# Seven quads of routed rows turned by loads from SBUF to SBUF, and expert outputs written to two PSUM banks in turn

## The chip, the core and the metric

The kernel is one program on 1 core of a Trainium2 chip. The metric is device time in microseconds (us), from one launch to its end. Each kernel is run several times, and the median counts.

The engines are TensorE (PE; PEld is its weight loads), VectorE (DVE), ScalarE (ACT), GpSimd (POOL) and SyncE (SP), which here only issues DMAs. Each engine takes its own instructions in order and waits on semaphores. A name with a q behind it (SPq) is that engine's queue of instructions that start DMAs or set registers.

## What is computed

The input x is 32 sequences of 125 tokens of 192 numbers. The reference does three things in a row:

- It scores each token (a product with `tok_w`) and keeps the best 88 of 125 in each sequence, in order of score: 32 x 88 = 2816 rows.
- It adds quantized attention of the layer-normed rows: q, k and v from one matrix, 12 heads of 16, scores quantized to steps, a softmax that gives powers of two, a projection, all of it rounded to steps.
- It adds a mixture of experts of the layer-normed rows: they are normed once more and scaled, a gate picks 4 of 16 experts for each row with softmax weights, each expert is 192 -> 384 -> gated unit -> 192, and the four outputs are summed with their weights.

Float products are made from fp16 pairs, a high part and the rest (low part), so one product takes several matmuls.

## The kernel before, in words

**Front part** (about 0 to 130 us). x is loaded, scored, ranked, and gathered into `xsel` (24 tiles of 128 rows, `NT` = 24; three tiles are a *quad* of four sequences, `NQ` = 8). Meanwhile SP fills `region` in DRAM with empty rows (`fill_rows`, L480 to L484: 45 stores of 800 KB) and loads the weights of experts two by two (`load_pair`, L464 to L478). SP's order is written out at L493 to L499: for m from 2 to 8 it issues some fills, waits on `stage_low` and loads pair m. The last 11 fills belong to m = 4.

**Attention part** (to about 445 us). It is a pipeline of slots, one per tile (`tile_slots`, `slot(st, n, q)` in each engine's program). In a slot, DVE runs the softmax of one tile (L1381 to L1466), ACT its half of it (L961, L988, L1009, L1015), PE the scores of the next tile and the output of the one before. Work for whole quads hangs in certain slots: q, k and v of the next quad, and behind it the routing of the quad that is through attention. For quad q the routing steps sit in slots 3q+5 (`COEFFS`) to 3q+9 (`SEND`):

- `NORM`, slot 3q+6: ACT writes the normed rows as fp16 high parts into `rows[q % 3]` (L894, L899).
- `TURN`, slot 3q+7: POOL adds the low parts (`low_rows`, L335 and L336, semaphore `low2`). PE then turns the rows by nine transposes of 128x128 into PSUM, in two lots (`turn_rows`, L1715 to L1724: two tiles, then one). DVE copies each lot to `xTr` in SBUF (`evac_rT`, L1294 to L1303). ACT copies 64 of its partitions to `tEr` (`last_rows`, L901 to L906).
- `GATE`, the same slot, at its end: PE makes the gate's logits from `xTr` and `tEr` with 15 matmuls (`gate_rows`, L1726 to L1738). DVE picks the four experts (`top_experts`, L1305 on, its first instruction is L1309).
- `RANK` and `SEND`: the place of each row in its expert's list, and 12 indirect stores per quad from POOL, each of which writes the rows of one tile and one choice to `region`.

PE's matmuls for q, k, v, turning and gate all use PSUM bank `pX` one after another. The order is made by `fill_order` (L345 on): fill n may start when drain n-1 is through (`xr_filled`, `xr_drained`). In a `TURN` slot the order is: turn lot 0, turn lot 1, `("qk", 4)`, gate, `("qk", 5)`. ACT drains a `qk` fill with L878, and in its program the drain of `("qk", 4)` stands behind `last_rows`. It has L1009, the softmax step that DVE's next slot needs, right behind that. Quad 7 (`LASTQ`) is turned inside the expert part, through bank `pO`.

**Expert part** (to about 726 us). Rows of `region` are taken in 59 steps (`NS`) of 256 rows of one expert, again as a pipeline of slots (`step_slots`). In slot st:

- SP loads step st: a transposing load of 256 x 384 numbers of 2 bytes from DRAM (L527) and a small load (L529), up to 8 steps ahead.
- PE makes the hidden values of step st-2 in three groups of five matmuls (L1904: hidG, hidC, hidL), then the output of step st-5 in ten (L1920) into `y_ps`, one half of bank `pX`.
- ACT starts with moving the output of step st-6 out of `y_ps` (L1044, semaphore `y_out`), then applies the gating function (L1049, L1052), then makes fp16 parts (L1059, L1061) and copies `tEb` (L1067) for later steps.
- DVE clips and multiplies (L1593, L1600), makes low parts (L1577, L1578), and computes where rows go. POOL scatters the output rows to `expert_rows` by two indirect stores per step (L782).

PE waits before L1920 until the output before has left the bank (L1915: `y_out` >= p - 5), and before the first L1904 of a step for `te_copied`, `l_done` (DVE's L1593) and `gs_ready` of two steps earlier (L1896 to L1898).

**Last part.** `expert_rows` is loaded back, weighted, summed and stored.

Of the kernel before, what the change touches and what calls it, by code (L numbers as in the profile page):

```python
# [64 lines left out]
def audio_tower(nc, x, tok_w, tok_b, w_qkv, b_qkv, w_proj, b_proj, sw_qkv, sw_proj, s_a1, s_attn,  # L65
                s_a2, s_a3, ffn_scale, gate_w, gate_b, w1, b1, w2, b2, out):
    ctx = ExitStack()
    with ctx:
# [19 lines left out]
        def carve(shape, dt, size):  # L88
# [212 lines left out]
        y_ps = pX[:, 0:2 * C].rearrange("p (j c) -> p j c", j=2)  # L301
# [9 lines left out]
            dve_chain root2 var2 ssq2 base_ready shift2 norm2 high2 low2 tT_drained ter_copied coeffs  # L311
# [36 lines left out]
        def fill_order():  # L348

            order = []  # L350
            for st in range(LAST):
                i, nxt = st % 3, st // 3 + 1 < NQ
                if nxt:
                    order += [(st, "qk", 1)] if i == 1 else [(st, "v", 0)] if i == 2 else [(st, "x", 0), (st, "x", 1)]
                    order += [(st, "qk", 2), (st, "qk", 3)] if i == 1 else []
                if nxt and i != 1:
                    order += [(st, "x", 2)] if i == 0 else [(st, "v", 1)]
                if quad_at(st, RANK) is not None:
                    order += [("rank", quad_at(st, RANK))]
                if quad_at(st, TURN) is not None:  # L360
                    order += [("rows", quad_at(st, TURN), m) for m in range(2)]
                if nxt and i == 1:
                    order += [(st, "qk", 4)]
                if quad_at(st, GATE) is not None:
                    order += [("gate", quad_at(st, GATE))]
                if nxt and i < 2:
                    order += [(st, "qk", 5 * i)]
            return {name: 11 + n for n, name in enumerate(order)}
# [26 lines left out]
        def turned(q):  # L395

            return rT_ps if q < NQ - 1 else rT_last

# [16 lines left out]
        ROUTE_CONSTS = 38  # L415
        WIDEN_AT = 2
# [13 lines left out]
        def _(sp):  # L430
# [62 lines left out]
            sp.wait_ge(s["route_consts"], ROUTE_CONSTS)  # L493
            for m in range(2, E // 2 + 1):
                for f in range(*((0, 24) if m == 2 else (24, 34) if m == 3 else (34, NFILL) if m == 4 else (0, 0))):
                    fill_rows(f)
                if m < E // 2:
                    sp.wait_ge(s["stage_low"], 12 * (m - 1))
                    load_pair(m % 2, 2 * m)  # L499

# [294 lines left out]
        def _(act):  # L795
# [105 lines left out]
            def last_rows(q):  # L901

                act.wait_ge(s["tT_drained"], 2 * q + 2)
                if q >= 1:
                    act.wait_ge(s["xr_filled"], fill("gate", q - 1) + 1)
                act.activation(tEr[0:CB, :], xTr[0:CB, 2, :], ACT.Copy).then_inc(s["ter_copied"], 1)  # L906
# [130 lines left out]
            def gate_values(st, p, it):  # L1037
                r, u = st % 2, st % UNROLL
                b = (st - 6) % 4
                if active(st, 6):  # L1040
                    act.wait_ge(s["mm2_done"], p - 5)
                    if st >= 10:
                        act.wait_ge(y_sent[b], it * 64 + 32 * ((u - 6) // 4))
                    act.activation(ysb[b], y_ps, ACT.Copy, scale=1.0 / (XS * WS * WS)).then_inc(s["y_out"], 1)  # L1044
# [50 lines left out]
        def _(dve):  # L1095
# [198 lines left out]
            def evac_rT(q, m):  # L1294

                dve.wait_ge(s["xr_filled"], fill("rows", q, m) + 1)
                if q >= 1:
                    dve.wait_ge(s["ter_copied"], q)
                dst = xTr[:, :, 0:256] if m == 0 else xTr[:, :, 256:384]
                dve.tensor_copy(dst, turned(q)[m]).then_inc(s["xr_drained"], 1)  # L1300
                if m == 1:
                    dve.wait_ge(s["xr_drained"], fill("rows", q, m) + 1)
                    dve.sem_inc(s["tT_drained"], 2)  # L1303
# [71 lines left out]
            def slot(st, n, q):  # L1375
# [60 lines left out]
                if quad_at(st, TURN) is not None:  # L1436
                    evac_rT(quad_at(st, TURN), 0)
# [5 lines left out]
                if quad_at(st, TURN) is not None:  # L1443
                    evac_rT(quad_at(st, TURN), 1)
# [177 lines left out]
        def _(pe):  # L1622
# [92 lines left out]
            def turn_rows(q, m):  # L1715
# [3 lines left out]
                for i in ((0, 1), (2,))[m]:  # L1719
                    src, cols = rows[q % 3][:, i, :], slice(128 * (i % 2), 128 * (i % 2) + 128)  # L1720
                    for kind, lo in enumerate((0, 2 * CA, CA)):
                        ins = pe.transpose(turned(q)[m][:, kind, cols], src[:, lo:lo + 128], idh[:, :])
                ins.then_inc(s["xr_filled"], 1)

            def gate_rows(q):

                pe.wait_ge(s["ter_copied"], q + 1)
                pe.wait_ge(s["tT_drained"], 2 * q + 2)
# [4 lines left out]
                for i in range(3):  # L1733
                    cols = slice(128 * i, 128 * i + 128)
                    for n, (lhs, kind) in enumerate(((xTr[:, 0, cols], 0), (xTr[:, 0, cols], 1), (xTr[:, 1, cols], 0),
                                                     (xTr[:, 2, cols], 2), (tEr[:, cols], 3))):
# [38 lines left out]
            def slot(st, n, q):  # L1775
# [34 lines left out]
                if quad_at(st, TURN) is not None:  # L1810
                    for m in range(2):
                        turn_rows(quad_at(st, TURN), m)
# [77 lines left out]
            def products(st, p, it):  # L1890
# [16 lines left out]
                if active(st, 5):  # L1907
# [5 lines left out]
                    pe.wait_ge(s["ave_ready"], p - 4)  # L1913
                    if st >= 6:
                        pe.wait_ge(s["y_out"], p - 5)  # L1915
                    for j in range(2):
                        tok = slice(128 * j, 128 * j + 128)
                        for n, (lhs, kind) in enumerate(((av[g][:, 0, tok], 0), (av[g][:, 0, tok], 1), (av[g][:, 1, tok], 0),
                                                         (av[g][:, 2, tok], 2), (avE[g][:, tok], 3))):
                            ins = pe.matmul(y_ps[:, j, :], lhs, w2s[:, kind, bass.ds(k_, 1), :].rearrange("p o f -> p (o f)"),  # L1920
# [45 lines left out]
```

## Time and profile before

| | |
|---|---|
| runs | 757.69, 760.58, 761.43 us; median 760.58 |
| the profiled execution: its own time | 765.98 us |
| its span (first to last instruction) | 764.2 us |
| mean granted TensorE clock | 0.685 |
| busy, share of the span | DVE 73%, ACT 64%, POOL 59%, PE 58% |
| chain that ended last, by engine | PE 22%, ACT 18%, SPq 17%, DVE 17%, issue 12%, another core or an unknown queue 6%, POOL 4% |
| DMA queues | SP's 139266 packets, 75.04 MB; POOL's 10272 packets, 17.70 MB |

Busy is the time in which an engine had an instruction under way. "Idle before" an instruction is put down to whatever released it ("<-"); "issue" means that the profile shows no wait. The granted clock is 1.00 at full speed and 0.50 at half. The sum of the prediction is made against the profiled execution, and its difference is applied to the median.

### The profile page before, as it was taken

What the parts mean: (1) busy time and instruction counts of PE and PEld (TensorE: products, weight loads), DVE (VectorE), ACT (ScalarE), POOL (GpSimd) and SP (SyncE); (2) the same over time, 40 slices, a digit from 0 to 9 for tenths busy, and PEclk for the clock granted to TensorE, in tenths of its full rate; (3) what the DMA queues carried; (4) which work ended last, traced back from release to release, by engine and by line L of the source; (5) the groups of instructions that cost most, each with busy time, mean ns of one, the idle gap of its engine ahead of it and who ended that gap; (6) DMA issues with size and microseconds to landing.
All of it is one profiled execution on the core that took longest, in us unless ns stands there. A gap on an engine that the chain in (4) does not pass through costs nothing.

```text
span 764.2 us, 14352 instructions
## 1 busy us (share of the span) xinstructions
PE 441.1 (58%) x3943; PEld 294.3 (39%) x3943; DVE 560.7 (73%) x1426; ACT 490.9 (64%) x874; POOL 447.3 (59%) x554
## 2 busy tenths in 40 slices
PE   0695353746456463745633335567687787788454
PEld 0242132333334242433422224345465565466343
DVE  3686897899999999898998645545676665666746
ACT  0055876798897969788774535255666655666664
POOL 9781725247587987979777653555455444445500
PEclk9997555555555555555555567679999988979669
DMA  9469999999011030210101164425444344431078
GB/s 186 55 145 293 318 318 294 321 293 285 13 55 53 22 93 30 79 40 6 51 11 40 52 102 86 101 72 126 97 92 93 83 95 86 91 81 34 1 291 317
DMA packets 149613, 93.65 MB, mean 123 GB/s; under 512 B 77122, under 2 KB 143643, under 8 KB 149538
## 3 DMA queue, kind: packets, MB, share of 16 engines
q1 hardware_dynamic: 139266, 75.04, 38.7%
q0 software_dynamic: 10272, 17.70, 7.3%
q8 instruction: 36, 0.59, 0.3%
q14 instruction: 39, 0.32, 0.2%
HBM read 23.61 MB, written 61.24 MB: 111 GB/s over the span
## 4 chain that ended last, share of the span: by engine, by line
PE 22%; ACT 18%; SPq 17%; DVE 17%; issue 12%; another core or an unknown queue 6%; POOL 4%; DMA 2%; DVEq 0%; ACTq 0%; POOLq 0%
SPq L483 7%; PE pX L1920 6%; PE pS L1904 6%; PE pP L1904 4%; SPq L475 3%; POOL w1s L597 2%; DVE S_e L1462 2%; ACT stage L1059 2%; DVE negmx L1381 2%; SPq L537 2%; DMA w2s<-expert_rows 2%; SPq L432 2%; PE pP L1796 1%; ACT stage L1044 1%
## 5 line engine op out<-in xcount | busy, mean ns | idle before, releaser
L782 POOL DMA_INDIRECT expert_rows<-stage,dest x118 | 118.6, 1005 | 130.3 <-ACT stage L1044 74.4
L1593 DVE TENSOR_SCALAR arena<-pS 128x512 f32<-128x512 f32 x59 | 40.6, 689 | 80.7 <-remote 59.9
L1920 PE MATMUL pX<-w2s,stage 128*128 x472 | 65.1, 270 | 39.8 <-ACT stage L1044 32.1
L706 POOL DMA_INDIRECT region<-rows,slots x60 | 68.0, 1134 | 16.5 <-issue 15.9
L597 POOL TENSOR_TENSOR w1s<-stage,w1s 128x384 f16<-128x384 f32 (+8 forms) x72 | 67.3, 935 | 11.4 <-ACT w1s L866 6.4
L1920 PEld LDWEIGHTS pX<-w2s,stage 128*128 128x128 f16 x472 | 43.6, 106 | 57.3 <-issue 53.6
L1052 ACT ACTIVATE arena<-pS 64x256 f32<-64x256 f32 x59 | 22.1, 375 | 59.5 <-PE pP L1904 30.1
L1796 PE MATMUL pP<-idb,S_p 128*88 128x128 bf16 x192 | 25.8, 316 | 46.3 <-DVE S_p L1414 46.3
L1674 PE MATMUL pX<-arena,WA 128*128 128x384 f16 x86 | 34.4, 501 | 30.5 <-ACT arena L878 21.2
L1823 PE MATMUL pP<-WpT,oq 128*128 128x192 bf16 x72 | 15.4, 349 | 60.7 <-ACT pTs L996 57.7
L706 POOL DMA_INDIRECT region<-arena,slots x36 | 41.0, 1138 | 15.6 <-issue 8.5
L961 ACT ACTIVATE S_g<-S_w,kf 128x1056 int16<-128x1056 uint16 x24 | 30.3, 1264 | 23.5 <-DVE S_w L1386 23.5
L752 POOL CAST oq<-o 128x384 bf16<-128x384 int8 x24 | 20.8, 865 | 41.3 <-ACT o L971 41.3
L1904 PE MATMUL pS<-arena,w1s 128*128 128x256 f16 x224 | 38.2, 293 | 8.3 <-issue 8.2
L878 ACT ACTIVATE arena<-pX,qkB,qkA 128x384 int8<-128x384 f32 x43 | 28.6, 665 | 22.1 <-PE pX L1674 16.3
L1044 ACT ACTIVATE stage<-pX 128x384 f32<-128x384 f32 x59 | 27.9, 473 | 22.6 <-remote 16.3
L1462 DVE SCALAR_TENSOR_TENSOR S_e<-S_sq,kf,S_pow 128x1056 f32<-128x1056 f32 x24 | 33.6, 1398 | 11.9 <-ACT S_sq L988 9.8
L1796 PEld LDWEIGHTS pP<-idb,S_p 128*88 128x88 bf16 x192 | 21.9, 191 | 51.6 <-DVE S_p L1414 49.5
L1049 ACT ACTIVATE arena<-pP 128x256 f32<-128x256 f32 x59 | 21.9, 371 | 26.9 <-remote 19.3
L1697 PE MATMUL pS<-arena 32*96 32x88 bf16 (+1 forms) x576 | 33.3, 276 | 7.6 <-ACT S_u L886 4.0
L1904 PE MATMUL pS<-tEb,w1s 128*128 128x256 f16 x118 | 35.4, 300 | 3.8 <-issue 3.8
L1422 DVE SCALAR_TENSOR_TENSOR S_rho<-S_g,kf,S_w 128x1056 int16<-128x1056 int16 x24 | 35.7, 1486 | 1.1 <-ACT S_g L961 1.1
(442 smaller groups left out, 1620.7 us busy)
## 6 DMA issues: line engine op xcount, KB each, us to landing
region<-zrow SPq DMA_DIRECT2D x45, 800.0 KB
w1s<-expert_rows SPq DMA_DIRECT2D x16, 384.0 KB, 7.7
stage<-in_L_ffn_w_dram SPq DMA_DIRECT2D x24, 192.0 KB
stage<-in_L_ffn_w_dram SPq DMA_DIRECT2D x8, 384.0 KB
w2s<-expert_rows SPq DMA_DIRECT2D x8, 384.0 KB, 11.8
arena<-in_x_dram SPq DMA_DIRECT2D x4, 672.0 KB
expert_rows<-stage,dest POOLq DMA_INDIRECT x118
out_dram<-xsel SPq DMA_DIRECT2D x8, 198.0 KB
```

Of the source, the lines that this page charges most:

```text
L483: sp.dma_start(region_rows[FILL * f:FILL * f + FILL].rearrange("(p j) c -> p j c", p=128), zrow[:, 0:ROW].unsqueeze(1).broadcast_to([128, ...
L597: pool.tensor_tensor(ws[rows, min(kind + 1, 3), two, to:to + width], st[rows, :, at:at + width], ws[rows, kind, two, to:to + width], ALU.s ...
L706: pool.indirect_dma_start(region_rows, bass.IndirectOffsetOnAxis(ap=slots[q % 3][:, i, m:m + 1], axis=0), rows[q % 3][:, i, :].bitcast(I16 ...
L782: pool.indirect_dma_start(y_dram, bass.IndirectOffsetOnAxis(ap=dest[(st - 7) % 8][:, j:j + 1], axis=0), ysb[b][:, j, :], None, bounds_chec ...
L1044: act.activation(ysb[b], y_ps, ACT.Copy, scale=1.0 / (XS * WS * WS)).then_inc(s["y_out"], 1)
L1422: dve.scalar_tensor_tensor(S_rho[:, :, :], S_g[:, :, :], k(K_X), S_w[:, :, :], ALU.mult, ALU.subtract).then_inc(s["rho_ready"], 1)
L1462: dve.scalar_tensor_tensor(S_e[:, :, :], S_sq[:, :, :], k(K_KK), S_pow[:, :, :].bitcast(BF16), ALU.add, ALU.mult).then_inc(s["e_ready"], 1)
L1593: dve.tensor_scalar(lin[r], hidLC[r], -6.0 * XS * WS, 8.0 * XS * WS, ALU.max, ALU.min).then_inc(s["l_done"], 1)
L1674: ins = pe.matmul(bank[:, 0:384], W[:, 128 * c:128 * c + 128], xT[:, kind, :], start=kind == 0, stop=kind == 2)
L1796: ins = pe.transpose(pP[0:KEEP, 0, 128 * h:128 * h + 128], S_p[:, h, :].bitcast(BF16), idb[:, :])
L1904: ins = pe.matmul(dst, w1s[:, kind, bass.ds(k_, 1), 128 * window:128 * window + 128].rearrange("p o f -> p (o f)"), rhs, start=n == 0, sto ...
L1920: ins = pe.matmul(y_ps[:, j, :], lhs, w2s[:, kind, bass.ds(k_, 1), :].rearrange("p o f -> p (o f)"), start=n == 0, stop=n == 4)
```

## The change

1. **Turning.** For quads 0 to 6 PE's nine transposes and DVE's two copies are dropped. In their place SP issues three transposing loads from `rows[q % 3]` in SBUF to `xTr` in SBUF, one per tile of 128 rows and 384 columns (`turn_by_load`). SP waits for `low2` first. In SP's program the call for quad m-4 stands ahead of the load of expert pair m (for m from 4 to 8), and the last two stand behind that loop. ACT's `last_rows` and PE's `gate_rows` wait on the new semaphore `turned` in place of `tT_drained`. The fills of `pX` for turning drop out of the order. Quad 7 stays as it was.
2. **Layout.** The loads write the columns in their order, so the second and third plane of `xTr` change places everywhere.
3. **Two banks.** The expert output of step n goes to bank `pO` for odd n from 7 on, and to `pX` otherwise. From step 8 on PE waits for `y_out` of the output before the last (p - 6), not of the last. Step 7 also waits until quad 7 is through with `pO` (`own_ready` >= 2).

```diff
+        y_banks = [bank[:, 0:2 * C].rearrange("p (j c) -> p j c", j=2) for bank in (pX, pO)]
+        def y_ps(n):
+            return y_banks[n % 2 if n >= Y_APART else 0]
...
-                if quad_at(st, TURN) is not None:
+                if quad_at(st, TURN) is not None and quad_at(st, TURN) == NQ - 1:
                     order += [("rows", quad_at(st, TURN), m) for m in range(2)]
...
+        Y_APART = SPREAD_AT
...
+            def turn_by_load(q):
+                sp.wait_ge(s["low2"], 2 * q + 2)
+                if q >= 1:
+                    sp.wait_ge(s["xr_filled"], fill("gate", q - 1) + 1)
+                    sp.wait_ge(s["ter_copied"], q)
+                for i in range(3):
+                    sp.dma_start(xTr[:, :, 128 * i:128 * i + 128], rows[q % 3][:, i, 0:2 * C],
+                                 transpose=True).then_inc(s["turned"], 16)
             for m in range(2, E // 2 + 1):
                 for f in range(*((0, 24) if m == 2 else (24, 34) if m == 3 else (34, NFILL) if m == 4 else (0, 0))):
                     fill_rows(f)
+                if m >= 4:
+                    turn_by_load(m - 4)
                 if m < E // 2:
                     sp.wait_ge(s["stage_low"], 12 * (m - 1))
                     load_pair(m % 2, 2 * m)
+            for q in range(E // 2 - 3, LASTQ):
+                turn_by_load(q)
...
             def last_rows(q):
-                act.wait_ge(s["tT_drained"], 2 * q + 2)
+                if q < LASTQ:
+                    act.wait_ge(s["turned"], 48 * q + 48)
+                else:
+                    act.wait_ge(s["tT_drained"], 2)
                 if q >= 1:
                     act.wait_ge(s["xr_filled"], fill("gate", q - 1) + 1)
-                act.activation(tEr[0:CB, :], xTr[0:CB, 2, :], ACT.Copy).then_inc(s["ter_copied"], 1)
+                act.activation(tEr[0:CB, :], xTr[0:CB, 1, :], ACT.Copy).then_inc(s["ter_copied"], 1)
...
-                    act.activation(ysb[b], y_ps, ACT.Copy, scale=1.0 / (XS * WS * WS)).then_inc(s["y_out"], 1)
+                    act.activation(ysb[b], y_ps(st - 6), ACT.Copy, scale=1.0 / (XS * WS * WS)).then_inc(s["y_out"], 1)
...
-                if quad_at(st, TURN) is not None:
-                    evac_rT(quad_at(st, TURN), 0)
...
-                if quad_at(st, TURN) is not None:
-                    evac_rT(quad_at(st, TURN), 1)
...
             def gate_rows(q):
                 pe.wait_ge(s["ter_copied"], q + 1)
-                pe.wait_ge(s["tT_drained"], 2 * q + 2)
+                if q < LASTQ:
+                    pe.wait_ge(s["turned"], 48 * q + 48)
+                else:
+                    pe.wait_ge(s["tT_drained"], 2)
...
-                if quad_at(st, TURN) is not None:
-                    for m in range(2):
-                        turn_rows(quad_at(st, TURN), m)
...
+                    if st - 5 == Y_APART:
+                        pe.wait_ge(s["own_ready"], 2)
                     if st >= 6:
-                        pe.wait_ge(s["y_out"], p - 5)
+                        pe.wait_ge(s["y_out"], p - 5 if st - 5 <= Y_APART else p - 6)
...
-                            ins = pe.matmul(y_ps[:, j, :], lhs, w2s[:, kind, bass.ds(k_, 1), :].rearrange("p o f -> p (o f)"),
+                            ins = pe.matmul(y_ps(st - 5)[:, j, :], lhs, w2s[:, kind, bass.ds(k_, 1), :].rearrange("p o f -> p (o f)"),
```

## Rows read from the trace of the kernel before

**Rows 1.** Table of stretches: us; busy us of each engine (instructions); PEclk, DMA, GB/s

```profile
190.00:445.00 255.00, 128.21 (x1508) 84.09 (x1508) 226.56 (x463) 193.74 (x271) 195.92 (x213) 0.50 0.14 42
517.00:712.00 195.00, 150.79 (x1195) 109.82 (x1193) 119.52 (x320) 122.57 (x286) 97.03 (x97) 0.91 0.40 86
```

**Rows 2.** Timeline in the TURN slot of quad 2: start us, us, engine, line, idle before

```profile
270.39 1.10 POOL L336 TENSOR_TENSOR rows<-tn,rows 128x384 f16<-128x384 f32 x1
...
271.54 0.82 PE L1722 MATMUL pX<-idh,rows 128*128 128x128 f16 x6
...
272.40 0.56 DVE L1300 COPY early<-pX 128x768 f16<-128x768 f16 x1 [0.70 <-PE pX L1722]
...
273.62 0.36 DVE L1300 COPY early<-pX 128x384 f16<-128x384 f16 x1 [0.40 <-PE pX L1722]
...
274.07 0.52 ACT L906 ACTIVATE tEr<-early 64x384 f16<-64x384 f16 x1 [0.67 <-issue]
...
274.29 1.50 DVE L1462 SCALAR_TENSOR_TENSOR S_e<-S_sq,kf,S_pow 128x1056 f32<-128x1056 f32 x1 [0.31 <-DVE early L1300]
...
275.21 0.67 ACT L878 ACTIVATE arena<-pX,qkB,qkA 128x384 int8<-128x384 f32 x1 [0.62 <-PE pX L1674]
...
276.20 0.27 PE L1737 MATMUL pX<-gws,early 128*128 128x16 f16 x4
...
276.60 0.17 PE L1737 MATMUL pX<-gws,tEr 128*128 128x16 f16 x1
...
277.00 0.20 DVE L1309 COPY arena<-pX 128x48 f32<-128x48 f32 x1
```

**Rows 3.** Timeline of SP's first loads of steps and of ACT's use of them

```profile
444.61 1.36 SPq L527 DMA_TRANSPOSE S_g<-region  x1
...
447.31 1.23 SPq L527 DMA_TRANSPOSE S_rho<-region  x1
448.75 0.60 SPq L529 DMA_DIRECT2D arena<-region  x1
449.80 1.25 SPq L527 DMA_TRANSPOSE S_pow<-region  x1
...
450.87 0.42 ACT L1067 ACTIVATE tEb<-S_rho 64x256 f16<-64x256 f16 x1 [0.51 <-DMA S_rho<-region]
...
455.99 0.42 ACT L1067 ACTIVATE tEb<-S_pow 64x256 f16<-64x256 f16 x1 [2.41 <-DMA S_pow<-region]
```

**Rows 4.** Table of stretches, the us after the first of these loads was issued

```profile
446.00:447.00 1.00, 0.00 (x0) 0.00 (x0) 0.90 (x10) 0.67 (x2) 0.00 (x0) 0.50 0.93 180
```

**Rows 5.** Timeline around the TURN slot of quad 0: SP, POOL and DVE

```profile
155.88 24.46 SPq L483 DMA_DIRECT2D region<-zrow  x11
180.85 5.88 SPq L475 DMA_DIRECT2D stage<-in_L_ffn_w_dram  x6
...
182.31 1.10 POOL L336 TENSOR_TENSOR arena<-tn,arena 128x384 f16<-128x384 f32 x1
...
188.58 0.20 DVE L1309 COPY arena<-pX 128x48 f32<-128x48 f32 x1
```

**Rows 6.** Timeline in the TURN slot of quad 5

```profile
402.51 1.02 POOL L336 TENSOR_TENSOR rows<-tn,rows 128x384 f16<-128x384 f32 x1
...
408.86 0.20 DVE L1309 COPY arena<-pX 128x48 f32<-128x48 f32 x1
```

**Rows 7.** Waits between 517 and 712 us: total us, times, longest us

```profile
PE pX L1920 <- ACT stage L1044: 20.0, 17, 2.9
```

**Rows 8.** Groups of ACT's instructions between 517 and 712 us, the one with most idle time

```profile
L1052 ACT ACTIVATE arena<-pS 64x256 f32<-64x256 f32 x48 | 18.0, 375 | 53.3 <-PE pP L1904 26.2 <-remote 14.5 <-PE pS L1904 11.9
```

**Rows 9.** Timeline of one such wait, with DVE's clip and the step behind it

```profile
575.38 0.69 DVE L1593 TENSOR_SCALAR arena<-pS 128x512 f32<-128x512 f32 x1 [1.32 <-PE pS L1904]
...
576.38 0.61 PE L1920 MATMUL pX<-w2s,stage 128*128 x4 [1.82 <-ACT stage L1044]
...
577.75 1.06 PE L1904 MATMUL pP<-S_pow,w1s 128*128 128x256 f16 x4
```

More of the change, by code:

```diff
@@ L300, in audio_tower @@
         hidLC = [pS[:, 2 * i:2 * i + 2, 0:STEP] for i in range(2)]
-        y_ps = pX[:, 0:2 * C].rearrange("p (j c) -> p j c", j=2)
+        y_banks = [bank[:, 0:2 * C].rearrange("p (j c) -> p j c", j=2) for bank in (pX, pO)]
+        def y_ps(n):
+            return y_banks[n % 2 if n >= Y_APART else 0]
         names = """inv_ready kf_ready pool_chain tok_loaded shift_loaded small_loaded pads_zeroed nat_loaded nat8 nat_wide zeroed wt_ps wt_done consts
@@ L310, in audio_tower @@
             o8_ready oq_ready proj_ready pr_a resid stats2
-            dve_chain root2 var2 ssq2 base_ready shift2 norm2 high2 low2 tT_drained ter_copied coeffs
+            dve_chain root2 var2 ssq2 base_ready shift2 norm2 high2 low2 tT_drained turned ter_copied coeffs
             spread root_ready
@@ L393, in tile_slots @@
                 slot(st, st, st // 3)
-        def turned(q):
-            return rT_ps if q < NQ - 1 else rT_last
         def experts_of(q):
@@ L1299, in evac_rT @@
                 dst = xTr[:, :, 0:256] if m == 0 else xTr[:, :, 256:384]
-                dve.tensor_copy(dst, turned(q)[m]).then_inc(s["xr_drained"], 1)
+                dve.tensor_copy(dst, rT_last[m]).then_inc(s["xr_drained"], 1)
                 if m == 1:
@@ L1720, in turn_rows @@
                     src, cols = rows[q % 3][:, i, :], slice(128 * (i % 2), 128 * (i % 2) + 128)
-                    for kind, lo in enumerate((0, 2 * CA, CA)):
-                        ins = pe.transpose(turned(q)[m][:, kind, cols], src[:, lo:lo + 128], idh[:, :])
+                    for kind, lo in enumerate((0, CA, 2 * CA)):
+                        ins = pe.transpose(rT_last[m][:, kind, cols], src[:, lo:lo + 128], idh[:, :])
                 ins.then_inc(s["xr_filled"], 1)
@@ L1734, in gate_rows @@
                     cols = slice(128 * i, 128 * i + 128)
-                    for n, (lhs, kind) in enumerate(((xTr[:, 0, cols], 0), (xTr[:, 0, cols], 1), (xTr[:, 1, cols], 0),
-                                                     (xTr[:, 2, cols], 2), (tEr[:, cols], 3))):
+                    for n, (lhs, kind) in enumerate(((xTr[:, 0, cols], 0), (xTr[:, 0, cols], 1), (xTr[:, 2, cols], 0),
+                                                     (xTr[:, 1, cols], 2), (tEr[:, cols], 3))):
                         ins = pe.matmul(experts_of(q)[:, i, :], lhs, gws[:, kind, :], start=n == 0, stop=n == 4)
```

## The prediction

> **What bounds the kernel now.** I read the table of stretches first, since the change touches two parts that have different limits. Between 190 and 445 us DVE is busy 226.56 of 255 us and PE only 128.21 [rows 1], so there a microsecond on DVE counts and one on PE doesn't. Between 517 and 712 us nobody is full: PE 150.79 of 195, ACT 122.57, DVE 119.52 [rows 1]. That part is bound by waits of one engine for another. Next I read the timeline of one `TURN` slot, engine by engine, to see what stands between POOL's low part and DVE's first gate instruction [rows 2]. Then SP's transposing loads, the only ones of their kind in the trace [rows 3], and the waits of the expert part [rows 7 to 9].
>
> **Part 1, what is removed.** In the slot of quad 2 DVE ends its work at 272.40 - 0.70 = 271.70, waits 0.70, copies 0.56, waits 0.40, copies 0.36, and starts L1462 at 274.29 [rows 2]. Between the copies stands 0.26 us of other work (272.96 to 273.62 - 0.40), which stays. So L1462 could start at about 272.0, 2.3 us earlier. Were that all, six such slots would give 14 us. PE's transposes (0.82 us for six) are on an engine with room and count nothing themselves.
>
> **Part 1, what takes its place.** DVE soon needs the gate's logits (L1309), and these now hang on three loads. Let L be the time from the end of POOL's L336 to the landing of the last. Behind the landing come, in order:
>
> - ACT's copy to `tEr`, 0.09 after its release (273.98 to 274.07) and 0.52 long.
> - ACT's drain of `("qk", 4)`, L878, 0.67. It stands behind `last_rows` on ACT and ahead of the gate in bank `pX`, so PE's gate waits for both. Before, it was done at 275.88, out of the way.
> - 0.06 to PE's start, 0.57 for the 15 gate matmuls (276.20 to 276.77), 0.23 to DVE.
>
> That is 2.14 us. L1309 came 277.00 - 271.49 = 5.51 us after POOL [rows 2], so the slot is as long as before when L = 5.51 - 2.14 = 3.37, and each microsecond above makes it longer by one. Below it the gain is at most 2.3.
>
> **What L is.** No load from SBUF to SBUF is in the trace. The nearest are SP's transposing loads from DRAM, of 256 rows where these have 128. SP spends 1.23 us on one, and 0.60 on a small plain load [rows 3]; between these ends I take 0.9 for half the rows. From the end of issue to use, one took 450.87 - 448.54 = 2.33 us [rows 3], with other stores about. But the first, issued until 445.97, had moved 180 KB of its 192 in the microsecond up to 447.0 [rows 4], and half the bytes should take half of that: I take 1.3 for the tail, between 1.0 and 2.33. So L = 0.05 + 3 x 0.9 + 1.3 = 4.05, with ends 0.05 + 3 x 0.6 + 1.0 = 2.85 and 0.05 + 3 x 1.23 + 2.33 = 6.1. One load among POOL's stores took 455.99 - 449.80 = 6.2 [rows 3]; a quad can meet that, all of them hardly.
>
> The Trainium skill ("DMA: Bandwidth & Descriptors", section on the anatomy of one DMA) gives a DMA a fixed cost of about 2.0 us, most of it the receipt of the last byte. By it the tail would be 2.0 in place of 1.3, and part 1 would cost about 4 us more than the sum below.
>
> **Part 1, the sum.**
>
> - Quads 1 to 4 are alike: 4 x (4.05 - 3.37) = +2.7.
> - Quad 0: SP issues the last of eleven fills of 800 KB at 180.3, one per 2.2 us (24.46 / 11), and DMA is full; its next six loads took 5.88 us to issue [rows 5]. The turning loads come at 183.4 behind this queue; I add 1.0 to L. The limit is 188.58 - 183.41 - 2.14 = 3.03. So 5.05 - 3.03 = +2.0.
> - Quad 5 has no `("qk", 4)` behind it: the limit is 408.86 - 403.53 - (2.14 - 0.67) = 3.86 [rows 6], so +0.2.
> - Quad 6 is turned after the last scores, where DVE has a long list of small instructions and loads have time: its two copies fall away, -0.9.
>
> Together +4.0 us. With L at its ends: 4 x (-0.52) + 0.8 - 1.0 - 0.9 = -3.2, and 4 x 2.73 + 4.1 + 2.2 = +17.2. SP's queue: the load of pair m now comes behind the turning of quad m-4, one slot later; its user comes two slots on, so nothing. What else waits on SP is out of this part. The swapped planes cost nothing, since it is the same bytes and the same instructions.
>
> **Part 2, two banks.** PE waits for ACT's L1044 before an output 17 times, 20.0 us in all [rows 7]. That is the most that can come back. Not all does. In one case PE waited 1.82 us until 576.38, and the next hidden values began at 577.75. Without the wait they could begin no earlier than DVE's L1593 ends, 575.38 + 0.69 = 576.07 [rows 9]: 1.7 us are saved on PE, and another wait is right behind. Whether that moves the end depends on ACT. ACT is the other half of the loop, and it idles 53.3 us before L1052, mostly for PE [rows 8], which says that earlier hidden values do help. But ACT is busy 122.57 of 195, and much of its idle time is released by nothing that the trace shows ("remote" 14.5), or comes after the matmuls seem long done. I take 40%, -8 us, with 0 and -20 as ends. ACT's read of the other bank costs the same. The new wait at step 7 (`own_ready`) is for a table that DVE makes in its slot 7, while PE asks for it in slot 12: nothing.
>
> **Sum.** 765.98 + 4.0 - 8 = 762.0 for the profiled execution. That one is 5.4 us above the median, so 760.58 - 4.0 = 756.6; I say 757. Half a per cent (3.8 us) is about what a measurement can tell from no change.
>
> **Rivals.**
>
> - *The loop opens up.* The two banks recover nearly all 20 us, and L is 3.4 or less. For it: L1052's idle time. Against it: the waits on DVE that stand right behind. -18 and 0: 743. Chance 0.17.
> - *The loads come late (slower).* One mechanism: L decides how long ACT stands in `last_rows`, and the gate, L878 and L1009 queue behind it, so DVE stands at L1309. The sum of part 1 is about 6 L - 20. It eats the 8 us at L = 4.7 and shows as slower at L = 5.3. For it: 2.33 us of tail and the 6.2 us load, POOL's stores go on in the same slots, and quad 0 meets the fills. Against it: the 180 KB in one microsecond. At L = 6.1 and -3 from part 2: +14, 775; at 5.3 to 6, about 768. Chance 0.28.
> - *The clock falls.* PE's granted clock is 0.91 in the expert part and 0.50 before [rows 1]; if waits are spread otherwise it may spend more time at 0.50, as in the last row of the wait I read, where four matmuls take 1.06 us [rows 9]. With 30 us more of it, and PE busy for three quarters (150.79 of 195), 22 us of work would take 22 more; PE's idle quarter hides much, and I count 8 to 12 behind the two banks' zero: 765 to 770. Chance 0.05. The Trainium skill ("TensorE: Matmul & The Clock Gate", section on psum-queue depth-cycling) tells of a kernel that cycles through banks and lets the clock oscillate; no row here shows it of this kernel.
> - *Nothing happens.* The wait on `y_out` only moves to `l_done`, and L is near 3.4: 758 to 763. Chance 0.10.
> - My forecast, 750 to 762, has 0.40.
>
> **How the numbers follow.** Of my forecast's 0.40 some 0.23 lies below 756.8; with the first rival faster has 0.40. The rest of it, the fourth rival and the edge of the second make 0.29 for the same. Slower: most of the second and the third, 0.31. The range from 741 to 773 leaves out the far ends of the first two rivals. My forecast's own range is 750 to 762.
>
> **What would show it.** In the trace after: SP's issue of a turning load (0.9 us) and the start of L906 less the end of L336 (4.1 us). DVE idle before L1309 in six slots, released by PE's gate, about 2.9 us each, and no idle time before L1462 for L1300. PE's waits for L1044 below 5 us, and new waits before L1904 for `tEb` or DVE. The stretch from 190 to 445 us some 4 us longer, the steps from 517 on some 8 us shorter. I am wrong if L906 starts within 3 us of L336, or after 6, or if the expert part stays as long while PE's waits for L1044 are gone.

## The result, and the profile after

| | before | after |
|---|---|---|
| runs, us | 757.69, 760.58, 761.43, 763.13 | 766.09, 769.05, 768.69, 767.93 |
| median, us | 761.0 | 768.31 |
| the profiled execution, us | 765.98 | 766.09 |
| its span, us | 764.2 | 764.4 |
| mean granted clock | 0.685 | 0.699 |
| SP's packets | 139266 | 148002 |

The ratio is 1.0095, with a 95% interval of 1.0052 to 1.0138: the change makes the kernel 7.3 us slower. The two profiled executions hide it. The one of before is 5 us above its median, the one of after 2 us below, so their spans are equal. They have to be compared by parts.

The table of stretches of after, with the columns of [rows 1]: the rest of the attention part, and the expert part.

```profile
190.00:459.00 269.00, 120.71 (x1472) 78.34 (x1472) 221.90 (x466) 193.98 (x273) 205.65 (x214) 0.53 0.17 48
531.00:716.00 185.00, 148.75 (x1218) 107.84 (x1216) 121.71 (x323) 126.06 (x290) 98.89 (x98) 0.94 0.45 89
```

DVE has 4.66 us less to do (221.90 for 226.56 in [rows 1]) in a stretch that is 14 us longer. The boundary that I take in both kernels is SP's first load of a step, and the end of the expert part is its first load of `expert_rows`. The timelines of SP, after:

```profile
458.54 1.22 SPq L543 DMA_TRANSPOSE S_g<-region  x1
...
727.86 8.93 SPq L553 DMA_DIRECT2D w1s<-expert_rows  x16
```

and before, where the first of the two stands in [rows 3] (444.61):

```profile
728.99 8.80 SPq L537 DMA_DIRECT2D w1s<-expert_rows  x16
```

So the front and attention parts are 13.9 us longer, and the expert part takes 269.3 in place of 284.4 us, 15.1 less. The sum was +4.0 and -8.

Timeline of the `TURN` slot of quad 2 after, against [rows 2]:

```profile
274.54 1.10 POOL L341 TENSOR_TENSOR rows<-tn,rows 128x384 f16<-128x384 f32 x1
...
275.66 3.83 SPq L503 DMA_TRANSPOSE early<-rows  x3
...
276.21 1.56 DVE L1477 SCALAR_TENSOR_TENSOR S_e<-S_sq,kf,S_pow 128x1056 f32<-128x1056 f32 x1
...
281.05 0.52 ACT L925 ACTIVATE tEr<-early 64x384 f16<-64x384 f16 x1 [3.48 <-DMA early<-rows]
281.48 0.65 ACT L894 ACTIVATE arena<-pX,qkB,qkA 128x384 int8<-128x384 f32 x1
...
282.28 0.26 PE L1755 MATMUL pX<-gws,early 128*128 128x16 f16 x4 [3.75 <-ACT arena L894]
...
283.13 0.21 DVE L1328 COPY arena<-pX 128x48 f32<-128x48 f32 x1 [4.07 <-PE pX L1755]
```

DVE starts its softmax step 0.57 us after POOL's end, as the copies are gone. (It was 2.80 us before.) Behind that step and one more (L1481) it stands for 4.07 us. ACT stands 3.48 us for the landing, and if 0.09 us lie between landing and start, as the prediction has it, the last load landed at 280.96. L is 280.96 - 275.64 = 5.32 us: 3.83 of issue (1.28 per load), 1.47 of tail. Behind it 2.17 us follow. The gate step comes 7.49 us after POOL, where it came 5.51. Read in the same way, L is 5.35, 5.30 and 6.15 us in quads 1, 3 and 4; in quad 4 SP took 4.82 us for its three loads.

The other slots: DVE's gate steps of the other six quads after, then those of before that [rows 2, 5, 6] don't hold (start us, us, idle before).

```profile
190.91 0.21 DVE L1328 COPY arena<-pX 128x48 f32<-128x48 f32 x1 [5.63 <-PE pX L1755]
...
236.99 0.21 DVE L1328 COPY arena<-pX 128x48 f32<-128x48 f32 x1 [4.06 <-PE pX L1755]
...
329.25 0.21 DVE L1328 COPY arena<-pX 128x48 f32<-128x48 f32 x1 [4.04 <-PE pX L1755]
...
375.95 0.21 DVE L1328 COPY arena<-pX 128x48 f32<-128x48 f32 x1 [4.63 <-PE pX L1755]
...
424.13 0.21 DVE L1328 COPY arena<-pX 128x48 f32<-128x48 f32 x1 [8.80 <-remote]
...
454.89 0.21 DVE L1328 COPY arena<-pX 128x48 f32<-128x48 f32 x1 [2.87 <-remote]
```

```profile
232.66 0.20 DVE L1309 COPY arena<-pX 128x48 f32<-128x48 f32 x1
...
321.31 0.20 DVE L1309 COPY arena<-pX 128x48 f32<-128x48 f32 x1
...
365.62 0.20 DVE L1309 COPY arena<-pX 128x48 f32<-128x48 f32 x1
...
442.00 0.21 DVE L1309 COPY arena<-pX 128x48 f32<-128x48 f32 x1 [3.94 <-remote]
```

After lags before by 2.3, 4.3, 6.1, 7.9, 10.3, 15.3 and 12.9 us at quads 0 to 6. Quads 1 to 4 add 8.0 us, quad 5 alone 4.9. Quad 5's slot:

```profile
412.81 2.01 POOL L341 TENSOR_TENSOR rows<-tn,rows 128x384 f16<-128x384 f32 x1
...
414.84 4.49 SPq L503 DMA_TRANSPOSE early<-rows  x3
...
420.93 0.52 ACT L925 ACTIVATE tEr<-early 64x384 f16<-64x384 f16 x1 [7.70 <-issue]
...
421.90 0.17 PE L1755 MATMUL pX<-gws,tEr 128*128 128x16 f16 x1
```

POOL's low part took 2.01 us where it took 1.02 [rows 6], SP 4.49 us for its three loads, and the last gate matmul is on record until 422.07, but DVE got it at 424.13. For that pause the profile names no cause ("remote").

In the expert part the waits that the two banks aimed at are gone but for one of 1.1 us. Waits of PE between 531 and 716 us (total us, times, longest us), where [rows 7] had 20.0 us for the output before:

```profile
PE pP L1919 <- issue: 14.2, 20, 2.0
PE pS L1919 <- issue: 6.8, 15, 0.9
...
PE pP L1919 <- ACT tEb L1086: 5.1, 5, 1.3
PE pX L1937 <- issue: 3.3, 10, 0.5
PE pO L1937 <- issue: 2.7, 3, 1.0
...
PE pO L1937 <- ACT stage L1078: 1.1, 1, 1.1
```

### The profile page after: what moved, and what is told of

Read it like the earlier page. It is cut to its first block and busy times, and to the rows that moved or that the text cites. A ratio compares the mean times of both kernels' runs of the same rounds, so it can differ in the third digit from the quotient of the medians.

```text
span 764.4 us, 14207 instructions
## 1 busy us (share of the span) xinstructions
PE 424.1 (55%) x3880; PEld 283.8 (37%) x3880; DVE 553.5 (72%) x1412; ACT 490.8 (64%) x874; POOL 458.1 (60%) x554
## 3 DMA queue, kind: packets, MB, share of 16 engines
q1 hardware_dynamic: 148002, 77.11, 41.0%
## 5 line engine op out<-in xcount | busy, mean ns | idle before, releaser
L722 POOL DMA_INDIRECT region<-rows,slots x60 | 69.9, 1165 | 16.4 <-issue 14.9
L722 POOL DMA_INDIRECT region<-arena,slots x36 | 43.9, 1220 | 13.3 <-issue 8.1
L710 POOL CAST arena<-arena 128x384 bf16<-128x384 int8 x42 | 27.3, 662 | 29.1 <-ACT arena L894 28.8
L1937 PE MATMUL pX<-w2s,stage 128*128 x264 | 35.7, 265 | 12.0 <-ACT stage L1063 7.6
L1919 PE MATMUL pS<-arena,w1s 128*128 128x256 f16 x224 | 35.9, 286 | 6.2 <-issue 6.1
L1838 PEld LDWEIGHTS pP<-WpT,oq 128*128 128x128 bf16 x72 | 6.5, 115 | 82.3 <-issue 77.4
```

The costliest lines, as they stand in the source:

```text
L722: pool.indirect_dma_start(region_rows, bass.IndirectOffsetOnAxis(ap=slots[q % 3][:, i, m:m + 1], axis=0), rows[q % 3][:, i, :].bitcast(I16 ...
L1919: ins = pe.matmul(dst, w1s[:, kind, bass.ds(k_, 1), 128 * window:128 * window + 128].rearrange("p o f -> p (o f)"), rhs, start=n == 0, sto ...
L1937: ins = pe.matmul(y_ps(st - 5)[:, j, :], lhs, w2s[:, kind, bass.ds(k_, 1), :].rearrange("p o f -> p (o f)"), start=n == 0, stop=n == 4)
```

## The experiments

They ran in four jobs, each with its own runs of the kernel before. That took 674.9, 674.7, 767.3 and 757.8 us in the four. So there are two conditions: one as in the first measurement (761.0), one 85 us quicker, and nearly all of the difference lies in the expert part. Some expectations below put it down to the chip. That isn't borne out: by the numbers on record the jobs ran on chips 14, 12, 8 and 12, so number 12 took 675 us in the second and 758 in the fourth. Ratios are to the kernel before in the same job; differences in us are between medians, unless said otherwise.

### Each part alone (first job, 675 us)

`e1_banks` is the kernel before with part 3 of the change, `e2_turn` the changed kernel with one bank:

```diff
-            return y_banks[n % 2 if n >= Y_APART else 0]
+            return y_banks[0]
-                        pe.wait_ge(s["y_out"], p - 5 if st - 5 <= Y_APART else p - 6)
+                        pe.wait_ge(s["y_out"], p - 5)
```

> The kernel before with part 3 of the change alone: expert outputs go to two banks in turn, PE and DVE turn all quads. My theory (part 1 costs about 14 us by a late landing, and the two banks give back about half of that in the median run): the stretch up to SP's first load of a step is as before (444.6 us in the profile of before), the steps are 7 to 15 us shorter, the median is 747 to 754, faster. The rival 'the two banks do nothing, the shorter steps in the profile after are a run's luck': 758 to 763.

> The change without its two banks: seven quads are turned by SP's loads, all expert outputs go to one bank. My theory: SP's first load of a step comes at 457 to 460 us, 14 us later than before, and nothing gives it back: the median is 772 to 778, a ratio of about 1.018 to the kernel before. The rival that the load only fills idle time and the loss is made elsewhere: 761 to 768, as the kernel before or the changed one.

`e1_banks`: 1.0001 (0.9989 to 1.0014). `e2_turn`: 1.018 (1.0162 to 1.0197), 12.2 us. Part 1 costs about what the first profiles said (first step load at 453.8 us, 441.2 in `e1_banks`), and the two banks were worth nothing here, where I had expected 7 to 15 us.

### What SP's time for a load depends on

```diff
-                for i in range(3):
-                    sp.dma_start(xTr[:, :, 128 * i:128 * i + 128], rows[q % 3][:, i, 0:2 * C], ...)
+                sp.dma_start(xTr[:, :, 0:128], rows[q % 3][:, 0, 0:384], ...)
+                sp.dma_start(xTr[:, 0:2, 128:256], rows[q % 3][:, 1, 0:256], ...)
+                sp.dma_start(xTr[:, 2:3, 128:256], rows[q % 3][:, 1, 256:384], ...)
+                for k in range(3):
+                    sp.dma_start(xTr[:, k:k + 1, 256:384], rows[q % 3][:, 2, 128 * k:128 * k + 128], ...)
```

> The changed kernel with the same bytes in six loads per quad in place of three: tile 0 in one of 384 columns, tile 1 in one of 256 and one of 128, tile 2 in three of 128. It tells what the 1.27 us of SP per load depend on. If SP's time goes by columns: 1.27, 0.85 and 0.42 us for 384, 256 and 128 columns, 3.8 us per quad as before, and the time stays at 766 to 770. If it is a fixed price per load: six times 1.27 = 7.6 us per quad, the copy to tEr comes 3.8 us later in each of six slots, and the time is 788 to 793.

One run: 710.1 us. Timeline of quad 1 in `e3_sizes`: 384 columns, 256, 128, then three of 128.

```profile
232.49 1.26 SPq L502 DMA_TRANSPOSE early<-rows  x1
233.79 1.24 SPq L503 DMA_TRANSPOSE early<-rows  x1
235.08 1.23 SPq L505 DMA_TRANSPOSE early<-rows  x1
236.35 3.78 SPq L508 DMA_TRANSPOSE early<-rows  x3
...
241.25 0.52 ACT L930 ACTIVATE tEr<-early 64x384 f16<-64x384 f16 x1 [6.99 <-DMA early<-rows]
```

The price is fixed per load, 1.23 to 1.26 us for 128 to 384 columns. The same bytes in six loads cost 35 us against the kernel before, where three cost 12; the 23 us between them are the six slots of 3.8 us that a fixed price gives.

### The queue behind the landing

`e7_late2` moves what queues behind the loads:

```diff
 ACT, slot():
-                if quad_at(st, TURN) is not None:
-                    last_rows(quad_at(st, TURN))
                 (drain of qk 4, L1028, L1034)
+                if quad_at(st, TURN) is not None and st < NT:
+                    last_rows(quad_at(st, TURN))
                 (drain of qk 5)
 DVE, slot(), behind S_w of the next slot:
+                if quad_at(st - 1, GATE) is not None and st < NT:
+                    top_experts(quad_at(st - 1, GATE))
```

> The changed kernel with nothing taken from the loads, but with what queued behind them moved out of the way: on ACT the drain of qk 4 and both softmax steps stand ahead of the copy to tEr, and DVE takes the gate's logits of quads 0 to 5 in the next slot, behind its S_w. If the loss is a wait for the landing (my theory), it goes: DVE's idle time before the gate falls from 4.1 us to under 1 in each slot, SP's first load of a step comes at 425 to 440 us, the median is 738 to 752. If the loss is contention of the loads with POOL's stores or with DVE's and ACT's work, the slots stay as long as in the changed kernel: 760 to 768.

1.0044 (1.0027 to 1.0061): 3.6 us over the kernel before in place of 12.4 (`f1_after`, below). In its slot of quad 2:

```profile
273.16 3.83 SPq L503 DMA_TRANSPOSE early<-rows  x3
...
278.52 0.52 ACT L925 ACTIVATE tEr<-early 64x384 f16<-64x384 f16 x1 [0.69 <-DMA early<-rows]
...
279.70 0.21 DVE L1332 COPY arena<-pX 128x48 f32<-128x48 f32 x1 [0.26 <-PE pX L1761]
```

The loads take as long as in the changed kernel and DVE waits 0.26 us (0.3 to 1.0 in quads 1 to 4, 1.5 in quad 0, 2.7 in quad 5). So most of the loss was the wait, not contention. I had expected a gain over the kernel before, and that didn't come.

### The second job (675 us): the changed kernel, and its cures one by one

> The changed kernel itself, beside the runs of its parts, since the time of the kernel before was 674.9 us there and 761.0 in the first measurement, with the difference in the expert part. If the two banks are worth nothing where the expert part takes 196 us (as they alone were: ratio 1.0001) and the loads cost 12 us: a ratio of 1.018 to the kernel before, 687 us at 674.9. If the banks give back what part 1 costs wherever both are there: 1.00 to 1.01.

1.0181 (1.0155 to 1.0208): the whole change costs as much as part 1 alone.

`f2_wide` turns a quad by one load. The rows of three tiles stand 512 columns apart, so that one load covers all, gaps included. The diff shows its core; buffers moved to make room, and POOL clears the gaps in quads 0 to 2:

```diff
-                for i in range(3):
-                    sp.dma_start(xTr[:, :, 128 * i:128 * i + 128], rows[q % 3][:, i, 0:2 * C], transpose=True)
+                sp.dma_start(xTw[:, :, :].bitcast(I16),
+                             wide_rows[q % 3][:, :, :].rearrange("p i c -> p (i c)")[:, 0:1408].bitcast(I16), transpose=True)
```

> The changed kernel with one turning load per quad in place of three: the rows of three tiles stand 512 columns apart in SBUF, and one load turns 1408 columns, of which 256 are gaps. SP's issue per load was 1.18 to 1.26 us for 384, 256 and 128 columns alike. If it is a fixed price per load, SP spends 1.3 us per quad in place of 3.8, the end of the bytes comes later by at most 1 us, and the copy to tEr starts 1.2 to 2.5 us sooner after the low part in each slot: 6 to 14 us off the changed kernel, a ratio of 0.998 to 1.009 to the kernel before. If SP's price goes by the bytes once a load is longer: 3.8 us again, a ratio of 1.018.

1.0055 (1.0037 to 1.0073), 8.5 us off the changed kernel. Its slot of quad 2:

```profile
272.80 1.10 POOL L342 TENSOR_TENSOR rows<-tn,rows 128x384 f16<-128x384 f32 x1
...
273.92 1.44 SPq L503 DMA_TRANSPOSE early<-rows  x1
...
277.51 0.52 ACT L931 ACTIVATE tEr<-early 64x384 f16<-64x384 f16 x1 [1.68 <-DMA early<-rows]
...
279.32 0.21 DVE L1337 COPY arena<-pX 128x48 f32<-128x48 f32 x1 [2.00 <-PE pX L1764]
```

L is 277.42 - 273.90 = 3.52 us here, and the gate step comes 5.42 us after POOL. It was 5.51 in the kernel before [rows 2], and the prediction put the break-even at L = 3.37. What this kernel still loses arises in quad 0, where SP's one load took 3.30 us to issue: against `e1_banks` (first job, turns by PE) its gate step is 3.3 us late at quad 0 (191.21 for 187.89) and 3.4 at quad 4 (368.29 for 364.88). Quads 1 to 4 cost nothing.

`f3_act` is ACT's order of `e7_late2` alone, `f4_all` the wide load, ACT's order and DVE's late gate together.

> The changed kernel with ACT's order alone altered: the drain of qk 4 and both softmax steps stand ahead of the copy to tEr. The gate then waits only for the copy: 0.67 us less behind the landing in five slots, and the two softmax steps (2.2 us) are done inside the wait. My theory gives 3 to 8 us off the changed kernel, a ratio of 1.006 to 1.013. If DVE were bound by something else: 1.018, no change.

> One wide load, ACT's altered order, and DVE's gate step one slot later, together with the two banks. With all three nothing waits for the landing: DVE has neither the two copies nor the wait, 1 to 2 us less than before in each of five slots. A ratio of 0.985 to 0.997 to the kernel before. If the chain of fills in bank pX or POOL takes over as the bound (in the run with three loads DVE waited up to 1.3 us per fill of v for it): 1.000 to 1.006.

`f3_act`: 1.0142 (1.0116 to 1.0168), 3 us off the changed kernel, at the edge of what I had expected. `f4_all`: 0.9994 (0.9981 to 1.0006), level with the kernel before. What holds it is the chain of fills of `pX`. Waits of DVE between 228 and 362 us in `f4_all`:

```profile
DVE arena L1273 <- PE pX L1714: 9.1, 6, 1.7
```

L1273 drains a fill of v; in `e1_banks` (turning by PE) the waits for v and for the turned rows were:

```profile
DVE early L1305 <- PE pX L1727: 3.7, 7, 0.7
DVE arena L1246 <- PE pX L1689: 3.0, 3, 1.0
```

The late gate holds the bank, v comes later by 6.1 us in three quads, and that takes most of what the missing copies give. That it is this which levels the two kernels is my reading; no run takes this wait away alone.

### The third job (767 us): the gate behind v, and half the scatters

In `g1_next` the gate's fill comes behind qk 5 and the first v, PE makes it behind the scores, and DVE takes it behind its first v. `g2_nextwide` is the same with one wide load.

```diff
 fill_order(), slot i == 2, behind ("v", 0):
+                if quad_at(st - 1, GATE) is not None and st <= NT:
+                    order += [("gate", quad_at(st - 1, GATE))]
```

> The changed kernel (three loads, two banks) with the whole gate of quads 0 to 5 one slot later: in bank pX's order it comes behind qk 5 and the first fill of v, PE makes it behind the scores, DVE takes it behind its first v, and ACT's copy to tEr stands behind its softmax steps. Nobody then waits for the landing, and no fill of v for the gate (that took 9.1 us in six waits of DVE between 228 and 362 us in the run with all three edits). My theory: DVE is free of the two copies and of the wait, 1.8 to 2.3 us per quad shorter than in the kernel before in five slots, whatever the loads cost in issue: SP's first load of a step at 428 to 434 us, a ratio of 0.980 to 0.990. If another chain bounds the slot at its old length (POOL, or ACT's drains of pX): 0.995 to 1.005.

> The same with one load per quad of 1408 columns. By my theory the landing is off the path in the run with three loads, so that this one gains nothing over it in quads 1 to 5, and at most 1 to 2 us in quad 6, which is still turned on the path: a ratio lower by 0.000 to 0.003. If the landing still bounds: lower by 0.010 or more.

`g1_next`: 1.0136 (1.0104 to 1.0167), a miss. `g2_nextwide`: 1.0093 (1.0062 to 1.0124); the intervals overlap, so what one wide load gives here is open. The slot of quad 2 in `g1_next`:

```profile
285.26 1.36 PE L1718 MATMUL pS<-arena 32*96 32x88 bf16 x24 [0.80 <-POOL arena L712]
...
286.95 0.17 PE L1761 MATMUL pX<-gws,tEr 128*128 128x16 f16 x1
...
290.03 0.21 DVE L1332 COPY arena<-pX 128x48 f32<-128x48 f32 x1 [4.97 <-remote]
```

The scores wait for POOL's cast of qk 5, the gate stands behind the scores, and then it reaches DVE 2.9 us after its recorded end, a pause as in quad 5 of after.

`h1_half` is the kernel before with one scatter per step (the odd rows' outputs aren't sent, `expert_rows` is zeroed first), `h2_halfbanks` the same with two banks:

```diff
-                    for j in range(2):
+                    for j in range(1):
                         pool.indirect_dma_start(y_dram, ...)
```

> The kernel before (one bank, turning by PE) with the second of POOL's two scatters per step left out (the outputs of the odd rows of each step are not sent, and expert_rows is filled with zeros beforehand). On this chip POOL is busy or between two scatters for 142.6 of 150 us in the expert part, so I hold that POOL hides the wait for the single bank. Relieved of half the scatters, the steps take 165 to 190 us in place of 196, bound by PE, and PE's wait for ACT's move of the output (6.5 us in ten waits with one bank) comes onto the path. If PE was the bound all along: 190 to 197 us.

> The same with two banks. If two banks help wherever POOL isn't the bound (my theory of why they gave 15 us in the first pair of profiles and nothing here): its expert part is 4 to 12 us shorter than that of the one-bank run with half the scatters. If the 15 us of the first pair came from something else: the two are equal within 2 us.

`h1_half` took 0.9246 (0.9211 to 0.9282) of the kernel before, `h2_halfbanks` 0.9219 (0.9189 to 0.925). The expert part was 213.4 and 210.0 us, outside both ranges of `h1_half`; the 3.4 us between them lie between the two answers that I had laid out for the banks. (The first step load came at 456.8 and 458.7 us, 12 to 15 later than in the profiles of the kernel before, as more of `expert_rows` is zeroed first.) The telling thing is the rate. POOL's scatters, PE's waits and the table of stretches, between 530 and 650 us in `h1_half`:

```profile
L785 POOL DMA_INDIRECT expert_rows<-stage,dest x43 | 43.2, 1004 | 77.6 <-ACT stage L1047 54.9 <-DVE dest L1607 18.8 <-issue 4.0
```

```profile
PE pX L1923 <- ACT stage L1047: 1.8, 5, 0.4
```

```profile
530.00:650.00 120.00, 116.53 (x1067) 87.57 (x1065) 106.95 (x290) 108.58 (x257) 42.67 (x43) 1.00 0.54 99
```

43 steps in 120 us are 2.79 us each, and PE is busy for 116.5 of the 120, at full clock: PE bounds this stretch. Where the kernel before takes 675 us, a step took as long with both scatters. The changed kernel there (`f1_after`), between 500 and 640 us:

```profile
L798 POOL DMA_INDIRECT expert_rows<-stage,dest x101 | 107.8, 1067 | 30.8 <-issue 26.8 <-ACT stage L1063 3.7 <-DVE dest L1619 0.3
```

```profile
500.00:640.00 140.00, 130.82 (x1181) 97.72 (x1180) 119.92 (x328) 123.56 (x287) 108.90 (x103) 0.99 0.59 121
```

101 scatters are 50.5 steps, 2.77 us each. Here POOL is in a scatter or between two for 107.8 + 30.8 = 138.6 of the 140 us, and PE is busy for 130.8. So both theories hold in part: POOL is full in the quick condition, and with half of POOL's work a step is no shorter since PE is full at the same height. That also fits the two banks' worth of nothing there: a wait of PE ends behind POOL's work anyway. The two were seen in different jobs, and no run takes work off POOL in the quick condition itself.

### The fourth job (758 us): the two parts again, now in the first condition

> The two banks alone once more. The chips differ in the expert part: on the chips where the kernel before takes 675 us a step takes 2.77 us and two banks were worth nothing (1.0001); where it takes 761 to 767 us a step took 4.10 us with one bank and 3.76 with two (one pair of profiles). My theory is that two banks save time only where PE has pauses that nothing in the profile explains: if the kernel before takes 760 to 770 us here, this one has a ratio of 0.985 to 0.993; if it takes 675, 1.000 again. The rival, that the difference between the two profiles of the first pair was one run's luck: 1.000 on either chip.

> The turning loads alone, one bank, once more. The attention part was 12 to 14 us longer on either kind of chip. If the kernel before takes 760 to 770 us here: a ratio of 1.016 to 1.021, and together with the two banks' gain it gives the changed kernel's 1.0095. If it takes 675: 1.018 as before.

> The kernel before itself, for a profile on the same chip as the two above: SP's first load of a step at 441 to 445 us on any chip; the step at 4.1 us with pauses of PE if this chip is of the first kind, 2.77 us if not.

| | ratio | first step load, us | expert part, us |
|---|---|---|---|
| `k3_before` | (one run, 758.49 us) | 443.38 | 278.3 |
| `k1_banks` | 0.9892 (0.9866 to 0.9918) | 443.21 | 271.3 |
| `k2_turn` | 1.0186 (1.014 to 1.0231) | 457.13 | 278.7 |

Here the two banks give 8.2 us by the ratio, 7.4 by the medians and 7.0 in the profile's expert part; the loads cost 14.1, 15.1 and 13.8 (first step load). Together that is 5.9 to 7.7 us slower; the changed kernel was 7.3. The table of stretches from 535 to 695 us, `k3_before` and then `k1_banks`:

```profile
535.00:695.00 160.00, 126.88 (x1011) 92.54 (x1009) 100.75 (x273) 103.79 (x242) 80.44 (x81) 0.91 0.44 89
```

```profile
535.00:695.00 160.00, 128.22 (x1063) 90.18 (x1062) 106.24 (x287) 108.62 (x251) 84.61 (x85) 0.97 0.43 88
```

81 scatters against 85 in 160 us, so 3.95 and 3.76 us per step. The waits of `k3_before` in that stretch:

```profile
DVE arena L1593 <- remote: 39.9, 16, 3.3
...
PEld pX L1920 <- issue: 27.4, 32, 2.5
...
PE pX L1920 <- ACT stage L1044: 12.1, 15, 2.0
```

In this condition PE pauses with nothing to wait for that the profile shows, and DVE gets results late. I read it so: after a pause ACT's move of the output is late as well, and PE waits for that on top. With two banks that second wait is gone (no such row in `k1_banks`). In the other condition PE waited 7.3 us in 140 for it with one bank (`e2_turn`), and none of it showed in the time.

`g3_behind` is `g1_next` with DVE's gate step behind S_p:

> As the run with the whole gate one slot later, but DVE takes the logits behind its S_p, not behind its first v. There the scores stood behind POOL's cast of qk 5 and the gate behind the scores, so that DVE stood up to 5.0 us before the gate. Here 2.5 us of softmax work stand in between. If the place on DVE was the fault: SP's first load of a step 8 to 15 us earlier than there (464.6 us), a ratio of 0.998 to 1.006. If it is PE's late scores themselves that hold the slot up: 1.010 to 1.014 as there.

0.9941 (0.9912 to 0.997), first step load at 448.23, 16.3 us earlier than in `g1_next`: the place on DVE was most of the fault. It is faster than the kernel before, and not by its turning, since the first step load comes 4.9 us later; `k1_banks` has the lower median (750.4 for 753.6 us), though the intervals touch. **The version to keep** is the kernel before with two banks alone: 0.9892 in one condition, level (1.0001) in the other.

## Why the prediction was wrong

**The step that failed** is the term of L. "Between these ends I take 0.9 for half the rows" put SP's time between a load of 256 rows (1.23) and a small plain load (0.60). It is 1.28 in these slots, and `e3_sizes` shows the same price for a third of the columns. Neither half the rows nor a third of the columns moves it, so a transposing load's own row (1.23) was the value to take, not one between it and another kind of load. Three loads made it 1.1 us per slot. With 1.23 L would have been 5.04, part 1 +10 by the formula 6 L - 20, and the whole sum +2 in place of -4. Part 1 measured 13.9 us, 9.9 above its sum: L at 5.32 accounts for 7.6 of that (6 x 1.27), and the rest lies in quads 0, 4 and 5, below.

- **Tail.** 1.3 was taken, 1.47 measured in quad 2. The trace is nearer to that estimate than to a tail of the 2.0 us of the Trainium skill ("DMA: Bandwidth & Descriptors", the anatomy of one DMA). But that section is on DMAs that GpSimd issues, and its fixed cost holds the setup as well, so what stands against it is the whole of one load, 1.28 + 1.47 = 2.75 us, which is above it.
- **Behind the landing.** 2.14 us said, 2.17 measured. The break-even of 3.37 was borne out by `f2_wide` (L = 3.52, slot 5.42 for 5.51, nothing lost in quads 1 to 4).
- **Quads 1 to 4.** 4 x 0.68 = 2.7 said, 8.0 measured. L was 5.32 in quad 2 for 4.05, nearly all from the issue. In quad 4 it was 6.15, as SP took 4.82 us for its loads; why isn't known.
- **Quad 0.** 2.0 said, 2.3 measured by DVE's clock, which is near by luck: the slot had begun 1.5 us early. From POOL's end to the gate step it grew from 5.17 to 9.04 us, 3.9 more. SP took 4.55 us for its loads there, and ACT's copy started at 189.04, 7.2 us after POOL. So L was 7.1, for 5.05.
- **Quad 5.** 0.2 said, 4.9 measured. L was 6.0, 2.2 over the limit; POOL's low part was 1.0 us longer; and the gate came 2 us late from PE. In the quick condition (`f1_after`) that last part was missing, and in `k2_turn`, in the first condition, it was there again. The prediction had no term for it.
- **Quad 6 and the rest.** -0.9 said (and left out of the sum for the upper end, which comes to +16.3, not +17.2); the lag falls by 2.4 at quad 6 and stands at 13.9 at the first step load, 1.3 less than at quad 5.
- **Part 2.** -8 said. `k1_banks` measured -7.4 to -8.2 in that condition; the 40% behind the -8 was a guess, so its nearness is partly luck. The 15.1 us of the first pair were partly the profiled execution of before, 5 us over its median. That the gain is nothing in a condition without PE's pauses wasn't foreseen.
- **The rivals.** "The loads come late" was what happened, by its own formula: 6 L - 20 at L = 5.3 gives +12, less 8. The chance of 0.28 was too low; "no load from SBUF to SBUF is in the trace" should have moved weight to the upper end. "The loop opens up" failed on L. The clock did not fall: in the expert part it was 0.94 for 0.91 [rows 1], and 0.97 for 0.91 with the banks alone. So the loss of clock that the Trainium skill ("TensorE: Matmul & The Clock Gate", psum-queue depth-cycling) tells of in a kernel that cycles through banks did not show here.

**What stays open** is where PE's pauses come from. They are there in some jobs and not in others, for the same kernel. A chip's number doesn't settle it. With half of POOL's scatters (`h1_half`) no wait is put down to "remote" between 530 and 650 us, where `k3_before` has 39.9 us of them on DVE between 535 and 695. But between 457 and 530 us `h1_half` has them too, one of 11.7 us on ACT. That suggests that the scatters have a part in the pauses, and shows neither that they are the cause nor by which path. Nor is it known why PE's gate reached DVE 2 us late in quad 5.

## What to carry to other kernels

Price a transfer by how many there are before pricing its bytes, and lay data out so that one transfer does for three. When work goes from an engine to a DMA, look for who stands behind the landing: here a 0.5 us copy on ACT held up a drain, the gate and DVE, and moving them gave back more than two thirds of the loss (12.4 to 3.6 us); ACT's order alone gave 3 us of it. Changes that gain in one part and lose in another should be timed apart: the two banks alone were the better kernel.

## What the hardware showed unasked

- SP's time to issue a transposing load from SBUF to SBUF is 1.23 to 1.28 us for 128, 256 or 384 columns of 128 rows, 1.44 for 1408, in the slots of quads 1 and 2. In quads 0, 4 and 5 of after, three loads took 4.55, 4.82 and 4.49 us, and the one wide load of `f2_wide` 3.30 in quad 0.
- The time from the end of issue to the landing (0.09 us before ACT's copy) went with the size of the last load: 241.16 - 240.13 = 1.0 us for 128 columns, 1.5 for 384, 2.1 for 1408.
- The kernel before took 675 or 758 to 767 us in different jobs. The first step load came within 4 us (441.2 in `e1_banks`, 444.6 in the first profile), and the expert part took 196 us in `e1_banks`, where banks were worth nothing, and 278 or 284 in the two profiles of the kernel before.
- Two engines can be full at one height: POOL at 2.77 us per step in `f1_after`, PE at 2.79 in `h1_half`, in different jobs. Taking work off one can then show nothing.
